# Two neighbouring scans of a selective state-space block as one instruction of 2048 elements

## The reference

```python
x = x + 0.5 * ffn(layernorm(x))          # per group of 512 tokens: (x @ W1.T + b1) @ W2.T + b2, no nonlinearity
x = x + ssm(layernorm(x))
x = x + 0.5 * ffn(layernorm(x))

# ssm, D_INNER = 512 channels, 16 states each, sequences of 2048 tokens, batch of 2
xz = x @ Wi.T + bi
u  = silu(causal_conv(x_in))             # 4 taps per channel
dt = softplus(x_in[..., :32] @ Wdt.T + bdt)
A  = -exp(A_log)
def step(h, (dt_t, u_t)):
    h = h * exp(dt_t * A) + dt_t * Bm * u_t
    y = sum over n of h * Cm
out = ys * silu(z) @ Wo.T + bo + x * mean(Dv)
```

## Time and profile before

| | us |
|---|---|
| median of 3 runs (lowest, highest) | 786.12 (785.98, 790.87) |
| profiled run | 788.75 |
| span of that profile | 786.9 |
| VectorE busy | 673.5 (86%) |
| TensorE busy | 645.0 (82%) |
| ScalarE busy | 602.0 (76%) |
| GpSimd busy | 305.1 (39%) |

### The profile page before, as it was taken

How to read it: one execution, slowest core, us unless ns; L and a number is a source line. 1 busy time by engine, 2 the same in 40 slices (tenths; PEclk the granted TensorE clock), 3 DMA queues, 4 the chain that set the end, 5 groups by cost and what they waited for, 6 DMA issues and landing times.

```text
span 786.9 us, 8285 instructions
## 1 busy us (share of the span) xinstructions
PE 645.0 (82%) x2912; PEld 332.3 (42%) x2912; DVE 673.5 (86%) x460; ACT 602.0 (76%) x1066; POOL 305.1 (39%) x188
## 2 busy tenths in 40 slices
PE   7857686979984999998886999995768998756967
PEld 5632332633441465544241574541213644312636
DVE  2437847699999998999999998999999999999680
ACT  2488858689887789989786999898788697673453
POOL 0107530134284756626457742729900054000030
PEclk9997887999998999999997999997978998986979
DMA  8342344270738060162736060434152513532001
GB/s 298 129 160 68 120 142 167 95 252 20 296 122 304 9 234 8 61 233 98 250 110 237 10 232 1 182 112 192 50 178 64 195 47 119 176 121 93 1 1 53
DMA packets 40010, 103.08 MB, mean 131 GB/s; under 512 B 4064, under 2 KB 13024, under 8 KB 39968
## 3 DMA queue, kind: packets, MB, share of 16 engines
q1 hardware_dynamic: 37408, 94.40, 32.8%
q10 hardware_dynamic: 2560, 8.14, 4.5%
HBM read 23.08 MB, written 4.19 MB: 35 GB/s over the span
## 4 chain that ended last, share of the span: by engine, by line
PE 33%; issue 25%; ACT 19%; POOL 14%; DMA 6%; DVE 3%; ACTq 1%; POOLq 0%; SPq 0%; DVEq 0%
ACT G L1052 7%; PE Y L1328 6%; PE MB L1295 5%; DMA XI<-XI 5%; PE MB L1352 5%; POOL MS L838 4%; PE MB L1254 3%; PE MB L1213 3%; PE MB L1273 3%; POOL X L831 3%; ACT XN L879 2%; DVE G L1172 2%; POOL XN L817 2%; ACT XI L972 2%; POOL LV L800 2%
## 5 line engine op out<-in xcount | busy, mean ns | idle before, releaser
L1052 ACT ACTIVATE G<-RD,COL 128x1024 f32<-128x1024 f32 (+1 forms) x288 | 279.7, 1042 | 88.0 <-PE Y L1328 84.3
L1172 DVE TENSOR_TENSOR_SCAN G<-G,STT,RV 128x1024 f32<-128x1024 f32 (+1 forms) x160 | 314.3, 2023 | 12.1 <-ACT G L1052 11.6
L1172 DVE TENSOR_TENSOR_SCAN G<-G,RV 128x1024 f32<-128x1024 f32 (+1 forms) x128 | 270.5, 2168 | 10.9 <-ACT G L1052 5.9
L1328 PE MATMUL Y<-G,RW 128*32 128x512 f32 x1024 | 140.7, 666 | 57.7 <-DVE G L1172 53.9
L791 POOL TENSOR_SCALAR LV<-LV 128x4 f32<-128x4 f32 x19 | 18.9, 996 | 318.4 <-ACT XN L879 318.1
L1295 PE MATMUL MB<-XI,DIAG 128*64 128x512 f32 x248 | 73.1, 724 | 29.1 <-DMA XI<-XI 29.1
L1328 PEld LDWEIGHTS Y<-G,RW 128*32 128x32 f32 x1024 | 27.7, 115 | 142.4 <-DVE G L1172 75.5
L831 POOL TENSOR_SCALAR X<-X,LV 128x256 f32<-128x256 f32 x32 | 86.8, 2722 | 0.8
L800 POOL TENSOR_TENSOR LV<-LV,HALF 128x4 f32<-128x4 f32 x24 | 49.2, 2051 | 64.9 <-DVE LV L1127 63.4
L1254 PE MATMUL MB<-MT,XF 128*128 128x256 f32 x256 | 63.6, 393 | 9.2 <-ACT XF L899 7.2
L838 POOL TENSOR_SCALAR MS<-MS,MV 128x256 f32<-128x256 f32 x12 | 34.9, 2912 | 79.5 <-DVE MV L1106 79.5
(11 more groups left out here) (88 smaller groups left out, 761.6 us busy)
## 6 DMA issues: line engine op xcount, KB each, us to landing
RD<-DW SPq DMA_DIRECT2D x60, 512.0 KB, 3.6
RV<-DW SPq DMA_DIRECT2D x60, 512.0 KB, 6.0
W<-in_w SPq DMA_DIRECT2D x48, 256.5 KB, 3.4
XI<-XI ACTq DMA_DIRECT2D x30, 256.5 KB, 5.6
X<-in_x SPq DMA_DIRECT2D x8, 512.0 KB, 5.7
out<-X SPq DMA_DIRECT2D x8, 512.0 KB, 3.0
G<-in_w SPq DMA_DIRECT2D x4, 513.0 KB, 8.7
RV<-in_w SPq DMA_DIRECT2D x4, 513.0 KB, 12.6
```

The costliest lines, as they stand in the source:

```text
L1052: eng.activation(G[:, i % NG, t0:t1], RD[:, q, t0:t1], ACT.Exp, scale=NAC[:, states(i):states(i) + 1]).then_inc(sems["exp"])
L1172: eng.tensor_tensor_scan(g, g, RV[:, (4 * k + q) % NR, t0:t1], STT[:, idx:idx + 1] if goes_on else 0.0, ALU.mult, ALU.add).then_inc(sems[" ...
L1328: ins = eng.matmul(Y[32 * q:32 * q + 32, 512 * h:512 * h + 512], RW[:, states(i + o), :], G[:, (i + o) % NG, 512 * h:512 * h + 512], start ...
```

## The change

In blocks 1, 2, 3, 8, 9, 10 and 11 (`paired`: one scan per unit, and a sequence's start), the scans of units s and s + 1, s even, are one instruction: the two G buffers and the two RV buffers are neighbours in memory and are taken as rows of 2048. It waits for the second unit's `exp` and `repw` too, and counts two on the semaphore `scan` when it ends. For the second unit to start from zero, its first decay has to be zero: column 0 of RD for q = 1 and 3 is set to 1e30 by a small ScalarE copy (`huge`), at the start and again after block 7, the `repd` DMAs of these q leave column 0 out in iterations 0 and 2, and the factor of `exp` is kept at -1e-20 or below. The scans of all other blocks stay as they were.

```diff
@@ schedule @@
     for stage in ("ones", "half", "calm", "warm", "b2q", "topc", "nae"):
         do(stage)
+    do("huge", 0)
...
                 until("repd", ko, n % 4, fed(ko, po))
                 do("exp", n)
+                if n == AT[7, 0, 15]:
+                    do("huge", 1)
...
+def paired(i):
+
+    k = UNITS[i][0]
+    return runs(k) == 1 and k // 4 % 2 == 0
...
@@ SyncE, repd @@
                         e.wait_ge("exp", AT[(*scanned(k - 1), 12 + q)])
+                    if k // 4 % 2 == 0 and q % 2 and t0 == 0:
+                        t0 = 1
                     eng.dma_start(RD[:, q, t0:t1], fourfold(DW[q:P:4, 0, t0:t1])
...
@@ GpSimd, half @@
                     eng.memset(ZERO[:, :], 0.0)
+                    eng.memset(START[:, :], HUGE)
...
@@ ScalarE @@
+                elif stage == "huge":
+                    n, = a
+                    e.wait_ge("half")
+                    if n:
+                        e.wait_ge("exp", AT[7, 0, 15])
+                    eng.activation(RD[:, 1:4:2, 0], START[:, :], ACT.Copy).then_inc(sems["huge"])
...
                     e.wait_ge("nac")
+                    e.wait_ge("huge", k // 8)
...
@@ VectorE @@
-                    eng.tensor_scalar(NAC, NAC, -1.0, None, ALU.mult).then_inc(sems["nac"])
+                    eng.tensor_scalar(NAC, NAC, -1.0, -LEAST, ALU.mult, ALU.min).then_inc(sems["nac"])
...
-                    g = G[:, i % NG, t0:t1]
-                    eng.tensor_tensor_scan(g, g, RV[:, (4 * k + q) % NR, t0:t1], STT[:, idx:idx + 1] if goes_on else 0.0,
-                                           ALU.mult, ALU.add).then_inc(sems["scan"])
+                    if paired(i):
+                        if q % 2 == 0:
+                            e.wait_ge("repw", k, q + 1, 0)
+                            e.wait_ge("exp", i + 1)
+                            g = G[:, i % NG:i % NG + 2, :].rearrange("p a n -> p (a n)")
+                            r = (4 * k + q) % NR
+                            eng.tensor_tensor_scan(g, g, RV[:, r:r + 2, :].rearrange("p a n -> p (a n)"), 0.0,
+                                                   ALU.mult, ALU.add).then_inc(sems["scan"], 2)
+                    else:
+                        g = G[:, i % NG, t0:t1]
+                        eng.tensor_tensor_scan(g, g, RV[:, (4 * k + q) % NR, t0:t1], STT[:, idx:idx + 1] if goes_on else 0.0,
+                                               ALU.mult, ALU.add).then_inc(sems["scan"])
```

More of the change, by code:

```diff
@@ L14 @@
 EPS = 1e-5
+HUGE, LEAST = 1e30, 1e-20
 TOP = 17.0
@@ L634, in build @@
         ZERO = sb("ZERO", [P, 3])
+        START = sb("START", [P, 2])
         TOPC = sb("TOPC", [P, 4])
```

## The result

The changed kernel takes 793.64 us (median of 13 runs, 790.91 to 795.32), the kernel before on the same chip 788.25 us (13 runs). The ratio is 1.0064, 95% interval [1.0043, 1.0084]: 5.4 us slower, inside the 1% by which the prediction divides its cases. The forecast was 793.0 us, made of +6.9 us on a median of three runs, 786.12 us; thirteen runs put that median at 788.25 us, so the time fits better than the difference does, and by luck.

A forecast was written before the change was run, and what follows sets the result against it. VectorE, busy 86%, was taken to bound the kernel, in a loop with GpSimd, TensorE and ScalarE. -2.2 + 4.0 + 2.4 + 2.2 + 0.5 = +6.9 us on 786.12 gave 793.0 us; range 784 to 799.

The forecast's parts named there:

- The scan: Scan pairs, blocks 1 to 3 and 8 to 11: 4.32 us start to start, 0.05 us saved each, 2.8 us for 56.
- A: Block 1: waits for the second RV copy and one more `exp` (1.07 us) are covered by later waits, costing nothing.
- B: Blocks 1 to 2: GpSimd's `msv` ends later beside pairs, delaying TensorE, ScalarE, then VectorE; 2.1 to 6.4 us, taken 4.0.
- C: Blocks 3 to 4: `mv` behind both scans, `msv` later, VectorE delayed at the `vnorm` at 279.78; 2.1 to 4.3, taken 2.4.
- D: Block 9: pairs ahead of or between `vnorm` steps delay GpSimd's statistics and VectorE; one more `exp` wait; 2.2 us (0 to 4).
- E: Elsewhere, a pair can wait up to 1.07 us for its second `exp`; half counted once, 0.5 us.
- At nothing: Small ScalarE copies into RD, one more GpSimd memset, 1023-element RD copies and later `repw` taken as covered, costing nothing.
- faster: Rival: GpSimd's delays are covered, all 56 pairs save 0.05 us and the 0.98 us gap closes; 782.3 us, chance 0.2.
- Two ends everywhere: Rival: B 6.4, C 3.8, D 4, E 0.5 us, TensorE's clock lower after longer waits; 798.6 us or more, chance 0.15.
- one end each: Rival: every GpSimd operation waits for one pair end, B 2.1 and C 1.6; +4.2 us, 790.3 us, chance 0.2.
- my own case: Main forecast, between one end each and Two ends everywhere: +6.9 us, 793.0 us, likeliest 790 to 797, chance 0.45.
- The signs named beforehand: Record near 4.4 us, block 1 `msv` 9.5 to 14, TensorE's wait 7 or more, VectorE idle before block 2, longer `vnorm` waits.

The follow-up runs named there:

- the measurement by itself: No network: four GpSimd additions of [128x256] beside VectorE idle or scanning in pieces of 1024, 2048, 4096, or 2048 with a PSUM operand; first addition 5.15, 9.41, 17.95 us.
- own waits: Changed kernel's order, each pair two scans of 1024 with separate waits and counts; against the kernel before 787.76 us, ratio 1.0009; again 788.60 us, 1.0024.
- four at once: Changed kernel with four units together in blocks 2, 3, 8, 9, 11; against the kernel before: one 4096 scan 811.68 us (1.0302), four of 1024 799.56 us (1.0152).
- 20 clear pairs: Changed order, scans of 1024 with separate waits, but 20 pairs without urgent GpSimd work beside them as one 2048 scan; 787.06 us, ratio 1.0000 to the kernel before.

## Why the prediction was right, point by point

*The scan.* 4.32 us from start to start, as taken; the saving of 0.05 us a pair is too small to see.

*A, nothing:* right. Scan 12 of block 1 starts 0.19 us later.

*B, 4.0 taken, 2.5 measured.* Place and chain were right. The size was off: I put the first operation of `msv` between one end and two, by the earlier trace rows, and it was one end, near the low bound of 2.1. That was no chance of this execution: the operation takes 5.23 us in all five kernels with pairs there. Two ends do occur (5.15 us in the measurement by itself).

*C, 2.4 taken, 2.7 measured.* The size was right, the last link wasn't: VectorE lost it in front of scan 8 of block 4 (2.04 us for an `exp`), not at the `vnorm`. With short scans in the same order it is 0.2 to 0.6 us when `msv` of block 3 takes 5.47 us, so nearly all of it is length and not the moved `mv`. It is 1.9 us where that `msv` waits for two ends of 1024 (own waits), which is the same mechanism with short scans.

*D and E, 2.7 taken together, 2.4 measured* between scan 0 of block 8 and scan 0 of block 10 (the difference goes from +5.2 to +7.5 us). VectorE's waits in front of `vnorm` in this stretch add up to 5.5 us, and to 3.5 us in the kernel before, so D is 2.0 us of waiting (2.2 taken). E is 1.4 us, at scan 8 of block 8 (0.5 taken). Against them stand 0.8 us saved by 16 pairs and 0.3 us at block 10. The 1.40 and 1.69 us in front of `vnorm` are the same in three kernels with long scans and 0.03 us in the kernels of two scans with the pair's waits, so these two are of length. The third, 2.40 us, is 2.3 to 3.4 us in every kernel but those with four at once.

*At nothing:* wrong for the RV copies of block 10, where VectorE waited 1.64 us. The last two copies, issued beside two XI copies and a store of `out`, took 10.6 and 10.5 us to land, and 8.8 and 8.5 us in the kernel before. The fourth landed 6.1 us behind the start of scan 0. The pair 2, 3 wants it 4.4 us behind that start, scan 3 by itself 6.6 us. So the pair's wait for its second copy makes most of this, and the prediction had put that wait at nothing. It has nothing to do with length: with short scans and the same waits it was 1.55, 1.09 and 2.29 us, with own waits 0.98 and 0.22 us (0.55 us with 20 clear pairs), and there was none with the old order. The one trace in the new order without it has the full RD copies, so whether the copies of 1023 elements have a part in it stays open.

*What I left out* is at the end: from block 12 the difference shrinks by 1.8 us, with no long scan near. Of this 1.2 us is one wait of VectorE for an `exp` ahead of scan 12 in the first half of block 15, 3.12 us in the kernel before and 1.92 us in the changed one. It is 1.92 us in the kernel before with `msv` on VectorE too, and 3.13 and 3.22 us in two kernels with the new order. So it differs from trace to trace in either order, and is no gain of the change that these runs show. Its cause stays open.

*The sum.* With the 0.05 us of each pair in its stage, the prediction was +4.0 (B), +1.8 (to block 8), +1.1 (blocks 8 to 12) and nothing at the end. The profiles show +2.5, +2.5, +2.8 and -1.8, and +0.2 ahead of them: +6.2 us between the profiles, +5.4 us between the medians. The parts are off by up to 1.8 us each way and cancel. The mechanism was right; that the sum came within 0.7 us of the profiles is luck in part.

*Rivals.* With 1.0043 as its lower end, the interval excludes "faster". "Two ends everywhere" asked for B 6.4 and is out; "one end each", +4.2 us, had B right (2.1 for 2.5), C low (1.6 for 2.7), and was in total a little nearer to 5.4 us than my own case. The signs named beforehand came: record 4.45 us, `msv` 9.77 us (9.5 to 14), TensorE's wait 7.16 us (7 or more), VectorE idle 2.93 us ahead of block 2.

That blocks 8 to 12 lose by length is argued, not shown: the table doesn't separate long from short there. For the waits in front of `vnorm` it is shown, but these traces don't show that the kernel's time follows them. That B and C lose by length is shown in two ways, by two scans in the same order and by `msv` moved away; the clear pairs show that length costs nothing elsewhere, and 4096 that more length costs more.

## What to carry to other kernels

Joining two VectorE scans saved the fixed part of one, here 0.05 us. It also set how long a GpSimd operation stood still, since both operands lay in SBUF; so look first for a small GpSimd operation beside it that someone waits for, and join only where there is none, or give that operation to the busy engine (0.35 us there instead of up to 5.3 us; in the kernel before, that move cost 2.7 us in all). The share of time that GpSimd is busy tells nothing of this. It was 39%, 305 us; with each operation at the shortest that its form took in that trace it would be 122 us, so by this estimate more than half of it was waiting.

## What the runs showed that I had not expected

- A GpSimd operation issued just after the start of a scan let the next queued scan go first and took two ends in the measurement by itself: 5.15, 9.41 and 17.95 us at 1024, 2048 and 4096 elements. In the kernels it was one or two, always the same at one place of one kernel: the first operation of `msv` in block 1 took 5.16 us (two) in the kernel before and in three with own waits, 3.07 us (one) in both traces of two scans with the pair's waits, and 5.23 us (one) in all five with pairs. The scan had started 0.15 to 0.18 us earlier in each. What decides it stays open.
- Each operation let through cost VectorE about 0.2 us.
- With one operand in PSUM there was no hold: 1.13 us each beside scans of 2048, as with VectorE idle.
- The same 7.2 us wait of TensorE for `msv` went with 6.8 us at the lower clock in one trace and with 13.7 us in another, and that difference alone was 3 us. With scans of 4096 elements TensorE's mean granted clock was 0.889 to 0.902 over four runs, against 0.906 to 0.912 in the control of 1024.
